# Adjacency build in runs of three chunks instead of four, with TensorE's run counts loaded once per tile

## The chip, the cores and the metric

One core of a Trainium2 chip runs the whole program. Its engines are TensorE (PE, with its weight loads shown as PEld), VectorE (DVE), ScalarE (ACT), GpSimd (POOL) and SyncE (SP), each with its own instruction stream; they meet by semaphores. The metric is the device time in microseconds (us), the median of three runs, lower is better.

## The reference

The reference is a two-layer graph network on 3125 nodes with 256 features: in each layer a graph convolution over 100000 edges, an attention mix and an expert block. The part that matters here is the sum over edges, which every graph convolution does with the same edge list:

```python
dst = jnp.minimum((3125 * jax.random.uniform(k, (100000,)) ** 2.0).astype(jnp.int32), 49999)
_o = jnp.argsort(dst, stable=True)
src, dst = src[_o], dst[_o]
...
deg = jax.ops.segment_sum(jnp.ones_like(dst, jnp.float32), dst, num_segments=n)
dinv = jnp.where(deg > 0, jax.lax.rsqrt(deg), 0.0)
msgs = h[src] * (dinv[src] * dinv[dst])[:, None]
return jax.ops.segment_sum(msgs, dst, num_segments=n)
```

The edges are sorted by target, and the targets are drawn from a square, so low targets have many more edges than high ones.

## The kernel before

The kernel does not gather rows edge by edge. It first builds the dense matrix of edge counts (3125 x 3125, one count for each pair of target and source), writes it to DRAM as `adjacency`, and later uses it in plain matrix products. The build is one stage, near the start, between two barriers of all engines.

The 100000 edges lie in 782 chunks of 128 edges, one edge per partition. The targets lie in 125 groups of 25 nodes, and five groups make one of 25 tiles. A group needs every chunk in which one of its targets occurs. Because edges are sorted, these chunks are neighbours, so a group has a first chunk and a count. The kernel works them off in runs of `RUN` chunks: a group has as many runs as its chunks need, rounded up, at least one. These numbers depend on the data; they are made on the chip and kept in `ranges_row` as four words for each group: first chunk, runs, runs of all groups before, runs up to and with this one. Each engine reads them into registers (`ranges_of`, L469) and loops over the runs.

For one chunk, two one-hot matrices are made: `hot_src` (128 edges x 125, the edge's source within its block, with a last column of ones) and `hot_key` (128 edges x 625, target within the group times source block). Their matrix product, 128x126 by 128x625 in two matmuls (512 and 113 columns), is added to the group's sums in PSUM. The engines split the work like this:

- POOL (L479) prepares the per-edge numbers of each run, `run_keys` and `run_srcs`, in a ring of 16 runs, so it may be 16 runs ahead.
- DVE (L501) makes `hot_key` for every chunk of a run and `hot_src` for all but the last. There is one slot per chunk of a run (`hot_src[:, j, :]`), and before slot j is written again TensorE must have used it (`hot_used`).
- ACT (L561) makes `hot_src` of the last chunk of a run in two operations, a square (L577) and a ReLU (L581), one group ahead of TensorE, and takes the sums of each finished group out of PSUM (`take_out`, L590).
- PE (L534) loads the group's words, waits until its PSUM bank is free, adds the self-loops with two matmuls (L545), and then does two matmuls for each chunk (L554).
- SP (L610) writes each group's counts to DRAM.

The order in each engine is as written. PSUM has four pairs of banks for five groups (`SUM_BANK`), and five buffers for the counts.

Of the kernel before, what the change touches and what calls it, by code (L numbers as in the profile page):

```python
# [15 lines left out]
ds = bass.ds  # L16
# [3 lines left out]
T = 25  # L20
P = N // T
G = 5
TG = T // G
# [2 lines left out]
HID = 512  # L26
E = 100000
CHUNKS = 782
RUN = 4
AHEAD = 16  # L30
CHUNKS_PAD = CHUNKS + RUN
GW = T * 25
# [14 lines left out]
OWNERS = 125  # L47
# [28 lines left out]
def graph_kernel(nc, a, out):  # L76
    with ExitStack() as top:
# [132 lines left out]
        with ExitStack() as phase:  # L210
# [9 lines left out]
            ranges_row = s("ranges_row", [1, OWNERS, 4], I32)  # L220
# [212 lines left out]
            with ExitStack() as build, nc.Block() as block:  # L433
# [35 lines left out]
                def ranges_of(engine, group):  # L469

                    why = "the ranges were clamped when they were made"
                    _, values = nc.values_load_multi_w_load_instructions(
                        ranges_row[0:1, ds(group, 1), :].rearrange("a g n -> a (g n)"), engines=[engine])
                    return (nc.s_assert_within(values[0], 0, CHUNKS, skip_runtime_bounds_check_because=why),
                            nc.s_assert_within(values[1], 1, CHUNKS // RUN + 1, skip_runtime_bounds_check_because=why),
                            values[2] & 0xFFFF,
                            values[3] & 0xFFFF)

                @block.gpsimd  # L479
                def _(pool):  # L480
                    with pool.Fori(0, T) as tile:
                        for k in range(TG):
                            group = tile * TG + k
                            first, runs, before, _ = ranges_of(mybir.EngineType.Pool, group)
                            with pool.Fori(0, runs) as i:
                                chunk = nc.s_assert_within(
                                    first + i * RUN, 0, CHUNKS_PAD - RUN, skip_runtime_bounds_check_because=(
                                        "a group's runs end with its last chunk, or a run after the first"))
                                n = before + i
                                at = nc.s_assert_within(n & (AHEAD - 1), 0, AHEAD - 1, skip_runtime_bounds_check_because=(  # L490
                                    "the mask leaves no other"))
                                alone(pool, hot_ready, n * RUN + RUN)
                                nc.gpsimd.tensor_tensor(
                                    run_keys[:, ds(at, 1), :].rearrange("p a j -> p (a j)"), edge_key[:, ds(chunk, RUN)],
                                    neg_group[:, ds(group, 1)].to_broadcast([128, RUN]), ALU.add).then_inc(run_made, 1)
                                nc.gpsimd.tensor_copy(run_srcs[:, ds(at, 1), :].rearrange("p a j -> p (a j)"),
                                                      src_low[:, ds(chunk, RUN)]).then_inc(run_made, 1)
                    pool.wait_ge(most_ready, 2)
                    nc.gpsimd.partition_all_reduce(deg_all[:], deg_most[:], 128, RMAX).then_inc(most_reduced, 1)
# [34 lines left out]
                @block.tensor  # L534
                def _(pe):
                    pe.sem_inc(hot_used, RUN)
                    with pe.Fori(0, T) as tile:
                        for k in range(TG):
                            group = tile * TG + k
                            _, runs, before, _ = ranges_of(mybir.EngineType.PE, group)  # L540
                            sums = psflat[0:P + 1, SUM_BANK[k] * 512:SUM_BANK[k] * 512 + GW]
                            pe.wait_ge(group_out, group + (TG + 1 - SUM_BACK[k]))

                            for b, e in ((0, 512), (512, GW)):
                                nc.tensor.matmul(sums[:, b:e], own_ident[0:P, k, :],  # L545
                                                 loop_blocks[0:P, ds(tile * -1 + (T - 1 + k * GW + b), e - b)],
                                                 start=True, stop=True, skip_group_check=True)
                            with pe.Fori(0, runs) as i:
                                for j in range(RUN):
                                    pe.wait_ge(hot_ready, (before + i) * RUN + (AHEAD * RUN + j + 1))  # L550
                                    if j == RUN - 1:
                                        pe.wait_ge(act_hot_ready, before + i + 2)
                                    for b, e in ((0, 512), (512, GW)):
                                        last = nc.tensor.matmul(sums[:, b:e], hot_src[:, j, :], hot_key[:, j, b:e],  # L554
                                                                start=False, stop=True, skip_group_check=True)
                                    last.then_inc(hot_used, 1)

                    pe.wait_ge(parts_summed, 1)
                    nc.tensor.transpose(ps[0:P, 7, 0:T], degree_row[:], ident[0:T, 0:T]).then_inc(deg_ready, 1)

                @block.scalar  # L561
                def _(act):
                    act.dma_start(xres[:], a["x"].rearrange("(t p) c -> p t c", p=P)).then_inc(x_landed, 16)
                    act.wait_ge(prepared, 2)
                    act.sem_inc(group_out, TG)
                    for k in range(TG):
                        act.sem_inc(stored[k], 16)

                    def make_sources(group):

                        first, runs, before, upto = ranges_of(mybir.EngineType.Activation, group)
                        with act.Fori(0, runs) as i:
                            act.wait_ge(act_hot_ready, before + i + 1)
                            chunk = nc.s_assert_within(
                                first + i * RUN + (RUN - 1), 0, CHUNKS_PAD - 1, skip_runtime_bounds_check_because=(
                                    "a group's runs end with its last chunk, or a run after the first"))
                            nc.scalar.activation(apart_sq[:], col_iota[:, 0:P], ACT.Square,  # L577
                                                 bias=src_low[:, ds(chunk, 1)], scale=-1.0).then_inc(squared, 1)
                            act.wait_ge(squared, before + i + 1)
                            act.wait_ge(hot_used, (before + i) * RUN + RUN)  # L580
                            nc.scalar.activation(hot_src[:, RUN - 1, 0:P], apart_sq[:], ACT.Relu,  # L581
                                                 bias=ones[:, 0:1], scale=-1.0).then_inc(act_hot_ready, 1)
                        return upto

                    def take_out(tile, k, upto):

                        group = tile * TG + k
                        act.wait_ge(stored[k], tile * 16 + 16)
                        alone(act, hot_used, upto * RUN + RUN)
                        nc.scalar.activation(counts[0:P + 1, k, :],  # L590
                                             psflat[0:P + 1, SUM_BANK[k] * 512:SUM_BANK[k] * 512 + GW],
                                             ACT.Copy, accum_out=row_edges[0:P + 1, ds(group, 1)]).then_inc(group_out, 1)

                    act.sem_inc(act_hot_ready, 1)
                    make_sources(0)
                    with act.Fori(0, T - 1) as tile:
                        for k in range(TG):
                            make_sources(tile * TG + k + 1)
                            _, _, _, upto = ranges_of(mybir.EngineType.Activation, tile * TG + k)
                            take_out(tile, k, upto)  # L600
                    for k in range(TG):
                        if k < TG - 1:
                            make_sources((T - 1) * TG + k + 1)
                        _, _, _, upto = ranges_of(mybir.EngineType.Activation, (T - 1) * TG + k)
                        take_out(T - 1, k, upto)
                    act.wait_ge(deg_ready, 1)

                    nc.scalar.activation(deg_sqrt[:], ps[0:P, 7, 0:T], ACT.Sqrt, bias=ones[0:P, 0:1]).then_inc(sqrt_ready, 1)
# [3057 lines left out]
```

## Time and profile before

| | |
|---|---|
| three runs | 4675.97, 4673.75, 4687.11 us; median 4675.97 |
| profiled execution, first to last instruction | 4665.5 us |
| median of the runs over that span | 10.5 us |
| the build stage, first to last L554 | about 571 us, 12% of the span |
| granted TensorE clock in that stage | 1.00 |
| runs / chunk places in the build | 276 / 1104 |

The page gives the profiled execution only as its span; the time outside the first and the last instruction is not in it, so spans are compared with spans and the difference is carried to the median. The stage is closed by a barrier on both sides, so what it gains or loses moves all that follows by as much.

### The profile page before, as it was taken

How to read it: one execution, taken by the hardware profiler on the slowest of the kernel's cores; microseconds unless marked ns; L12 is line 12 of the kernel's file. 1: busy time of each engine (PE TensorE's matmuls, PEld its weight loads, DVE VectorE, ACT ScalarE, POOL GpSimd, SP SyncE). 2: the span in 40 equal slices, each digit the busy share in tenths (PEclk: the TensorE clock that was granted, in tenths of full speed). 3: DMA queues.
4: the chain of work that ended last, by engine and by line, in shares of the span. 5: the costliest groups of instructions: out<-in, count | busy, mean ns of one | idle time of the engine just before them, and what ended most of it. 6: DMA issues, size and time to landing. Idle time of an engine off the chain costs nothing. (4 is left out here: it accounts for less than half of the span.)

```text
span 4665.5 us, 90783 instructions
## 1 busy us (share of the span) xinstructions
PE 3696.0 (79%) x23366; PEld 2634.7 (56%) x23367; DVE 2192.7 (47%) x5709; ACT 1348.5 (29%) x2983; POOL 739.5 (16%) x1224
## 2 busy tenths in 40 slices
PE   4888864899699989973464629859989899789998
PEld 2444433566388579651354416539879544457776
DVE  7888878888700221151263420270130677723333
ACT  2555532677700110320010203240000135233333
POOL 3222100000000000017423470200000466100000
PEclk9999975887799899986787859879999999989999
DMA  2111220323244024102010121224425100010000
GB/s 105 47 74 74 93 86 0 91 90 90 76 160 157 32 108 184 60 16 53 11 53 4 40 25 39 98 77 170 165 105 196 49 1 1 5 29 7 13 13 27
DMA packets 125733, 317.98 MB, mean 68 GB/s; under 512 B 43522, under 2 KB 76785, under 8 KB 111116
## 3 DMA queue, kind: packets, MB, share of 16 engines
q1 hardware_dynamic: 110404, 300.31, 18.5%
q0 software_dynamic: 11808, 9.68, 1.5%
q10 hardware_dynamic: 3404, 6.53, 0.4%
q8 instruction: 62, 1.02, 0.1%
q14 instruction: 55, 0.45, 0.0%
HBM read 244.21 MB, written 72.41 MB: 68 GB/s over the span
## 5 line engine op out<-in xcount | busy, mean ns | idle before, releaser
L554 PE MATMUL ps<-hot_key,hot_src 128*126 128x512 bf16 (+1 forms) x2208 | 416.9, 314 | 38.6 <-DVE hot_key L519 21.1
L519 DVE TENSOR_SCALAR hot_key<-col_iota,run_keys 128x625 bf16<-128x625 int16 x1104 | 393.7, 378 | 0.0
L2441 PE MATMUL ps<-xnT,ew 128*128 (+2 forms) x640 | 207.5, 479 | 206.7 <-issue 150.9
L1335 PE MATMUL ps<-gnn_u_thirds,near 125*128 125x256 bf16 x3000 | 334.7, 274 | 23.1 <-issue 23.1
L554 PEld LDWEIGHTS ps<-hot_key,hot_src 128*126 128x126 bf16 x2208 | 212.7, 136 | 234.2 <-DVE hot_key L519 171.7
L1335 PEld LDWEIGHTS ps<-gnn_u_thirds,near 125*128 125x128 bf16 x3000 | 329.7, 141 | 26.3 <-issue 24.7
L2441 PEld LDWEIGHTS ps<-xnT,ew 128*128 128x128 f32 x640 | 129.7, 210 | 279.2 <-issue 183.5
L2322 POOL DMA_INDIRECT rows_room<-node_table,src_idx x256 | 260.1, 1016 | 142.4 <-issue 142.4
L516 DVE TENSOR_SCALAR hot_src<-col_iota,run_srcs 128x125 bf16<-128x125 int16 x828 | 211.6, 256 | 97.4 <-PE ps L554 52.8
L863 PE MATMUL ps<-row_hot,slot_hot 128*128 128x512 f16 x1088 | 217.6, 351 | 3.1 <-DVE row_hot L1076 2.6
L2477 PE MATMUL ps<-table_thirds,rows_room 125*128 125x144 bf16 x1728 | 129.2, 232 | 113.9 <-issue 78.0
L2456 PE MATMUL ps<-ew,ehT 128*125 128x256 f32 x800 | 210.7, 409 | 0.0
L3620 DVE SCALAR_TENSOR_TENSOR xres<-ps,shares,xres 125x256 f32 x200 | 96.8, 484 | 239.5 <-PE ps L3585 218.6
L3574 PE MATMUL ps<-xnT,f 128*128 x640 | 185.5, 438 | 12.2 <-ACTq L3593 4.6
L1076 DVE TENSOR_SCALAR row_hot<-row_iota,row_of 128x670 f16<-128x670 int16 x544 | 189.4, 391 | 0.0
L2477 PEld LDWEIGHTS ps<-table_thirds,rows_room 125*128 125x128 bf16 x1728 | 114.2, 100 | 128.8 <-issue 128.4
L1335 PE MATMUL ps<-agg_u_thirds,near 125*128 125x257 bf16 x1500 | 175.4, 277 | 10.2 <-issue 9.7
L3574 PE MATMUL ps<-f_h1T,f 128*128 128x313 f32 (+1 forms) x640 | 180.1, 434 | 0.0
L3585 PE MATMUL ps<-fo,f_h2T 128*125 128x256 f32 x800 | 179.2, 379 | 0.0
L1335 PEld LDWEIGHTS ps<-agg_u_thirds,near 125*128 125x128 bf16 x1500 | 169.6, 141 | 16.6 <-issue 15.4
L1335 PE MATMUL ps<-gcn_u_thirds,near 125*128 125x256 bf16 x1500 | 166.6, 274 | 12.7 <-DVEq L1554 12.7
L3601 ACT ACTIVATE f_h1T<-ps,norm_shift,norm_scale 128x313 f32<-128x313 f32 (+1 forms) x160 | 98.0, 612 | 261.7 <-PE ps L3574 261.7
(570 smaller groups left out, 6651.9 us busy)
## 6 DMA issues: line engine op xcount, KB each, us to landing
near<-adjacency SPq DMA_DIRECT2D x80, 1562.5 KB, 6.6
adjacency<-counts SPq DMA_DIRECT2D x125, 312.5 KB, 2.2
own_in<-own_rows SPq DMA_DIRECT2D x34, 512.0 KB, 4.0
expert_rows<-rows_y SPq DMA_DIRECT2D x75, 125.0 KB
rows_room<-expert_rows SPq DMA_DIRECT2D x25, 375.0 KB
pair_in<-high_rows SPq DMA_DIRECT2D x34, 256.0 KB
pair_in<-low_rows SPq DMA_DIRECT2D x34, 256.0 KB
agg0a_adj<-adjacency SPq DMA_DIRECT2D x5, 1562.5 KB, 9.4
```

The costliest lines, as they stand in the source:

```text
L516: nc.vector.tensor_scalar(hot_src[:, j, 0:P], col_iota[:, 0:P], run_srcs[:, ds(at, 1), j:j + 1].rearrange("p a j -> p (a j)"), None, ALU.i ...
L519: nc.vector.tensor_scalar(hot_key[:, j, :], col_iota[:], run_keys[:, ds(at, 1), j:j + 1].rearrange("p a j -> p (a j)"), None, ALU.is_equal ...
L554: last = nc.tensor.matmul(sums[:, b:e], hot_src[:, j, :], hot_key[:, j, b:e], start=False, stop=True, skip_group_check=True)
L863: last = nc.tensor.matmul(ps[:, bank, 0:e - b], slot_hot[:, c % RING, :], row_hot[:, c % RING, b:e], start=False, stop=True, skip_group_ch ...
L1076: nc.vector.tensor_scalar(row_hot[:, c % RING, :], row_iota[:], row_of[i][:, c:c + 1], None, ALU.is_equal).then_inc(routes_made, 1)
L1335: last = nc.tensor.matmul(ps[:, j, 0:width], lead_tiles[BUF[j]][:, k, :], parts.thirds[:, k, i, :], start=(k == 0 and i == 0), stop=(k == ...
L2322: pool.indirect_dma_start(out=fetched[q][:, j, :], out_offset=None, in_=node_table, in_offset=bass.IndirectOffsetOnAxis(ap=src_idx[:, q, j ...
L2441: last = nc.tensor.matmul(ps[:, piece % 2, 0:n], w1[i][:, c, m * 128:(m + 1) * 128], xnT[:, c, ds(g * NG + first, n)], start=(c == 0), sto ...
L2456: last = nc.tensor.matmul(o, hT[:, c, j * P:(j + 1) * P], w2[i][:, c, :], start=False, stop=(c == 3))
L2477: last = nc.tensor.matmul(pick_bank(i, k, many)[:, slot * MIDS * HROW:(slot + 1) * MIDS * HROW], src_hot[i][0:P, tier, edges_of], table_th ...
L3574: last = nc.tensor.matmul(ps[:, piece % 2, 0:n], (w1, w2)[stage][i][:, c, m * 128:(m + 1) * 128], moving, start=(c == 0), stop=(c == 1))
L3585: last = nc.tensor.matmul(o, h2T[:, c, j * P:(j + 1) * P], wo[i][:, c, :], start=(c == 0), stop=(c == 1))
```

## The change

`RUN` goes from 4 to 3. With it go the number of slots for the one-hots (four to three), the share of ACT (one source one-hot in three, no longer in four), the number of runs of each group and the places that a group's chunks are rounded up to. TensorE reads its run counts no longer before each group but once for each tile, ten words in one load (`tile_runs_of`). ACT no longer loads the words of a group a second time before it takes the sums out: the count of all runs before group g + 1, which it has already, is the count up to group g.

```diff
-RUN = 4
+RUN = 3
...
+                def tile_runs_of(engine, tile):
+
+                    why = "the ranges were clamped when they were made"
+                    _, values = nc.values_load_multi_w_load_instructions(
+                        ranges_row[0:1, ds(tile * TG, TG), 1:3], engines=[engine])
+                    return [(nc.s_assert_within(values[2 * k], 1, CHUNKS // RUN + 1, skip_runtime_bounds_check_because=why),
+                             values[2 * k + 1] & 0xFFFF) for k in range(TG)]
...
                     with pe.Fori(0, T) as tile:
+                        counted = tile_runs_of(mybir.EngineType.PE, tile)
                         for k in range(TG):
                             group = tile * TG + k
-                            _, runs, before, _ = ranges_of(mybir.EngineType.PE, group)
+                            runs, before = counted[k]
...
-                        return upto
+                        return before
...
                         for k in range(TG):
-                            make_sources(tile * TG + k + 1)
-                            _, _, _, upto = ranges_of(mybir.EngineType.Activation, tile * TG + k)
-                            take_out(tile, k, upto)
-                    for k in range(TG):
-                        if k < TG - 1:
-                            make_sources((T - 1) * TG + k + 1)
-                        _, _, _, upto = ranges_of(mybir.EngineType.Activation, (T - 1) * TG + k)
-                        take_out(T - 1, k, upto)
+                            take_out(tile, k, make_sources(tile * TG + k + 1))
+                    for k in range(TG - 1):
+                        take_out(T - 1, k, make_sources((T - 1) * TG + k + 1))
+                    _, _, _, all_runs = ranges_of(mybir.EngineType.Activation, OWNERS - 1)
+                    take_out(T - 1, TG - 1, all_runs)
```

On TensorE, between the last chunk of a group and the first of the next group, the kernel before has (L554 is a chunk's matmul, L545 the self-loops' matmul, L548 the loop over runs, L472 the load of the words, ISA a register instruction):

```order
L554 MATMUL ps<-hot_key,hot_src 126x113
L548 REGISTER_ALU
L548 COMPARE_AND_BRANCH
L472 ISA
L472 TENSOR_LOAD ranges_row
L542 REGISTER_ALU
L545 ISA
L545 MATMUL ps<-loop_blocks,own_ident 126x512
L545 ISA
L545 MATMUL ps<-loop_blocks,own_ident 126x113
```

and the changed kernel, where lines stand nine further down (L563 is the chunk's matmul, L554 the self-loops'):

```order
L563 MATMUL ps<-hot_key,hot_src 126x113
L557 REGISTER_ALU
L557 COMPARE_AND_BRANCH
L551 REGISTER_ALU
L554 ISA
L554 MATMUL ps<-loop_blocks,own_ident 126x512
L554 ISA
L554 MATMUL ps<-loop_blocks,own_ident 126x113
```

Two instructions are gone, the address and the load; the load stands once, ahead of the first of five groups.

On ScalarE, from the last source one-hot of a group to the taking out of the group before it, the kernel before has (L581 the one-hot, L167 and L590 the waits and the copy):

```order
L581 ACTIVATE hot_src<-src_apart_sq,ones 128x125
L572 REGISTER_ALU
L572 COMPARE_AND_BRANCH
L472 TENSOR_LOAD ranges_row
L167 REGISTER_ALU
L167 ISA
L590 REGISTER_ALU
L590 ACTIVATE counts,row_edges<-ps 126x625
```

and the changed kernel:

```order
L590 ACTIVATE hot_src<-src_apart_sq,ones 128x125
L581 REGISTER_ALU
L581 COMPARE_AND_BRANCH
L167 REGISTER_ALU
L167 ISA
L599 REGISTER_ALU
L599 ACTIVATE counts,row_edges<-ps 126x625
```

The load between the two operations is gone.

## Rows read from the trace of the kernel before

**Rows 1.** The page: the costliest groups of the build stage.
```profile
L519 DVE TENSOR_SCALAR hot_key<-col_iota,run_keys 128x625 bf16<-128x625 int16 x1104 | 393.7, 378 | 0.0
L516 DVE TENSOR_SCALAR hot_src<-col_iota,run_srcs 128x125 bf16<-128x125 int16 x828 | 211.6, 256 | 97.4 <-PE ps L554 52.8
```

**Rows 2.** Windows: L554 over the stage (window, length, busy and count, clock, DMA).
```profile
59.00:630.70 571.70, 416.83 (x2208) 212.72 (x2208) 1.00 0.19 72
```

**Rows 3.** Windows: L545 over fifty groups of two runs (two matmuls a group).
```profile
257.05:471.34 214.29, 23.84 (x100) 12.87 (x100) 1.00 0.19 75
```

**Rows 4.** Timeline of PEld, two groups of two runs (start, length, [idle before]).
```profile
406.51 0.26 PEld L545 LDWEIGHTS ps<-loop_blocks,own_ident 125*126 125x126 bf16 x2 [1.20 <-issue]
407.05 1.01 PEld L554 LDWEIGHTS ps<-hot_key,hot_src 128*126 128x126 bf16 x8 [0.27 <-DVE hot_key L519]
408.46 0.19 PEld L554 LDWEIGHTS ps<-hot_key,hot_src 128*126 128x126 bf16 x2 [0.40 <-DVE hot_key L519]
409.73 0.19 PEld L554 LDWEIGHTS ps<-hot_key,hot_src 128*126 128x126 bf16 x2 [0.17 <-issue]
410.73 0.26 PEld L545 LDWEIGHTS ps<-loop_blocks,own_ident 125*126 125x126 bf16 x2 [0.81 <-issue]
411.26 1.01 PEld L554 LDWEIGHTS ps<-hot_key,hot_src 128*126 128x126 bf16 x8 [0.27 <-DVE hot_key L519]
```

**Rows 5.** Timeline of DVE in the same stretch.
```profile
407.85 0.26 DVE L516 TENSOR_SCALAR hot_src<-col_iota,run_srcs 128x125 bf16<-128x125 int16 x1 [1.10 <-PE ps L554]
408.31 0.25 DVE L516 TENSOR_SCALAR hot_src<-col_iota,run_srcs 128x125 bf16<-128x125 int16 x1
409.60 0.26 DVE L516 TENSOR_SCALAR hot_src<-col_iota,run_srcs 128x125 bf16<-128x125 int16 x1
412.06 0.26 DVE L516 TENSOR_SCALAR hot_src<-col_iota,run_srcs 128x125 bf16<-128x125 int16 x1 [0.71 <-POOL run_keys L493]
```

**Rows 6.** Timeline of PEld at the end: groups of one run.
```profile
625.33 1.02 PEld L554 LDWEIGHTS ps<-hot_key,hot_src 128*126 128x126 bf16 x8 [0.27 <-DVE hot_key L519]
626.72 0.26 PEld L545 LDWEIGHTS ps<-loop_blocks,own_ident 125*126 125x126 bf16 x2 [0.38 <-issue]
627.28 1.01 PEld L554 LDWEIGHTS ps<-hot_key,hot_src 128*126 128x126 bf16 x8 [0.30 <-DVE hot_key L519]
629.50 1.01 PEld L554 LDWEIGHTS ps<-hot_key,hot_src 128*126 128x126 bf16 x8 [0.27 <-issue]
```

**Rows 7.** Loads of words: L472, and one word at L1324 (ns min/median/max).
```profile
L472 ACTq TENSOR_LOAD <-ranges_row x250: 303/308/677, 49.9 to 630.6; - x125
L472 PEldq TENSOR_LOAD <-ranges_row x125: 328/334/533, 45.8 to 628.4; - x125
L472 PEldq FUSED_REGOPS  x100: 46/52/66, 91.6 to 628.3; - x100
L1324 PEldq TENSOR_LOAD <-many_edges x4: 306/315/323, 1282.6 to 3433.9; - x4
```

**Rows 8.** Timeline of ACT over one group of two runs.
```profile
404.58 0.69 ACT L590 ACTIVATE counts<-ps 126x625 f32<-126x625 f32 x1 [0.39 <-PE ps L554]
405.50 0.40 ACT L577 ACTIVATE src_apart_sq<-col_iota,src_low 128x125 bf16<-128x125 int16 x1
406.01 0.40 ACT L581 ACTIVATE hot_src<-src_apart_sq,ones 128x125 bf16<-128x125 bf16 x1
406.64 0.40 ACT L577 ACTIVATE src_apart_sq<-col_iota,src_low 128x125 bf16<-128x125 int16 x1 [0.22 <-ACT hot_src L581]
408.39 0.40 ACT L581 ACTIVATE hot_src<-src_apart_sq,ones 128x125 bf16<-128x125 bf16 x1 [1.36 <-PE ps L554]
409.18 0.69 ACT L590 ACTIVATE counts<-ps 126x625 f32<-126x625 f32 x1 [0.39 <-PE ps L554]
```

**Rows 9.** Timeline of POOL in the first group.
```profile
69.32 0.22 POOL L493 TENSOR_TENSOR run_keys<-edge_key,neg_group  x1 [0.66 <-DVE hot_key L519]
70.36 0.20 POOL L493 TENSOR_TENSOR run_keys<-edge_key,neg_group  x1 [0.68 <-DVE hot_key L519]
```

More of the change, by code:

```diff
@@ L569, in make_sources @@
                     def make_sources(group):
-                        first, runs, before, upto = ranges_of(mybir.EngineType.Activation, group)
+                        first, runs, before, _ = ranges_of(mybir.EngineType.Activation, group)
                         with act.Fori(0, runs) as i:
```

## The prediction

> **What bounds the kernel now.** I read the page first, then windows over the stage, then the waits and the timelines of its engines. Everything the change touches lies in one stage between two barriers; its 2208 matmuls lie in a window of 571.70 us at a granted clock of 1.00, the upper of the two levels (2.4 GHz) [rows 2]. So the forecast is the change of that window, and all that follows moves with it.
>
> No engine is full in it: VectorE works 394 us on `hot_key` and 212 us on `hot_src`, with overlap, and loses 97 us waiting before `hot_src`, most of it for TensorE [rows 1]. What repeats is a cycle through two engines. In a group of two runs TensorE's first chunk loads at 407.05; VectorE, which waited for that slot, starts the next run at 407.85, 0.80 later; the first chunk of that run loads at 408.46, 0.61 after VectorE's start; the last at 409.73, 1.88 after it; then TensorE needs 1.00 to the self-loops at 410.73 and 0.53 to the next first chunk at 411.26 [rows 4, 5]. The sum 0.80 + 1.88 + 1.00 + 0.53 is 4.21, the whole period of the group. While TensorE is between groups, VectorE has filled its slots and stands still. A further run in a group costs VectorE's own time, 407.85 to 409.60, 1.75 [rows 5]. The first group of a tile has 1.20 of idle time before its self-loops where others have 0.81, so 0.39 more [rows 4]; five groups then take 5 x 4.21 + 0.39 = 21.44, and fifty groups measure 214.29, 21.43 for five [rows 3]. A group of one run takes 1.95 or 2.22 [rows 6], I use 2.08.
>
> From the reference's edge list I count the chunks that each group touches. At four to a run that makes 276 runs, 1104 places, as in the trace [rows 1]: 25 groups of one run, 79 of two, 21 of more, with 51 runs beyond the second in all. The stage is then 100 x 4.21 + 25 x 2.08 + 51 x 1.75 + 24 x 0.39 = 421.0 + 52.0 + 89.3 + 9.4 = 571.6, against 571.7 measured. The same sum can be made for the changed kernel.
>
> **The change part by part.** Counts: at three to a run there are 345 runs, 1035 places. No group has one run any more: 84 have two, 41 have more, with 95 runs beyond the second.
>
> VectorE's run: one chunk with a source one-hot falls out, 407.85 to 408.31, 0.46 [rows 5]; its own time for a run is 1.75 - 0.46 = 1.29. The last chunk of a run comes 1.88 - 0.46 = 1.42 after its start.
>
> Slots: there are three, and the first is free again only by the round trip shown above: 0.61 from VectorE's start to TensorE's load, 0.80 from there to VectorE's next start, 1.41 together [rows 4, 5]. Under 1.75 that was hidden; over 1.29 it is not. A further run costs 1.41, a gain of 0.34 a run, but 0.47 for a chunk place where it was 0.44. The bounds are 1.29 and 1.75, and I take 1.41 since both halves are read from rows.
>
> TensorE's load: between groups the address (0.05) and the load (0.33) go [rows 7], 0.39 with rounding; the idle time there is 0.81 [rows 4], of which branch, wait and address of the self-loops stay. I take 0.50, 0.11 over the two durations for the sequencer's gaps, an estimate; the bounds are 0.39 and 0.81. The period of a group of two runs is 4.21 - 0.46 - 0.50 = 3.25. At the start of a tile the load stays, so that 0.50 is not saved there. It fetches ten words instead of four. One word takes 0.315 and four take 0.334 [rows 7], 0.006 a word, so I add 0.04; if the whole load grew with the words it would be 0.84, 0.50 more. A tile start costs 0.39 + 0.50 + 0.04 = 0.93 over 3.25.
>
> The Trainium skill, page "Runtime: NRT & Kernel Launch", section "Instruction fetch mechanics", says that such a load takes about 200 ns for each register. By it the ten words would take 2.0 us, and the sum would be some 39 us higher; four words would take 0.8, and the trace has 0.334.
>
> ScalarE: its cycle for a group of two runs without waits is, from taking out at 404.58, 0.92 to the square, 0.51, 0.63, again 0.51 to the second ReLU, and 0.79 (408.39 to 409.18) to the next taking out, 3.36 [rows 8]. For one run it is 0.92 + 0.51 + 0.79 = 2.22, just what the last one-run groups take [rows 6], so the chain is real. Without the load (0.31, with a gap 0.35, out of an idle time of 0.39 ahead of the taking out [rows 7, 8]) it is 3.01, below 3.25: ScalarE follows. If none of the load's time comes back it is 3.36, and 84 groups lose 0.11 each, +9 us; if it does, nothing. I take nothing, since the idle time before L590 has room for the load only. The freed 0.24 a group is all its slack; three-run groups have 3.01 + 1.14 = 4.15 against 4.66.
>
> GpSimd makes a run in 1.04 (69.32 to 70.36) [rows 9], below 1.41, and may be 16 runs ahead; even with one 0.32 load a group two runs fit into 3.25. SyncE's writes stay 125, at least 3.25 apart and into buffers five groups old. The shorter clearing of `hot_src` and the column fewer in the preparation lie beside GpSimd's start, at nothing; were they in the open it would be 0.2 us.
>
> The sum: 125 x 3.25 + 95 x 1.41 + 24 x 0.93 = 406.3 + 134.0 + 22.3 = 562.5, against 571.6: -9.1 us. Where it comes from: 59 groups keep two runs, -0.96 each, -57; 25 go from one to two, +1.17, +29; 20 go from two to three, +0.45, +9; 21 longer ones, -4; 24 tile starts, +0.54, +13. The large gain on the common group is mostly eaten by groups that need one run more. With 4665.5 for the span this gives 4656.4; the median of the runs lies 10.5 above the span, so 4676 becomes 4667.
>
> **Rivals.** A: three slots cost nothing, a further run takes 1.29. For it: TensorE catches up between runs with 0.27 a chunk when nothing is missing. Against it: 0.80 and 0.61 are in every group. Price 95 x -0.12 = -11, so 4656.
>
> B: ScalarE becomes the bound, as computed, +9, so 4676, no change. For it: it makes 345 pairs of operations instead of 276 and has 0.24 of slack a group; a slower start after a taking out (404.58 to 405.50) would use that up. Against it: the idle time of 1.36 before its ReLU [rows 8].
>
> C, the other side: TensorE's load was beside other work and its removal gives nothing between groups. In one-run groups the idle time before the self-loops is 0.38, not 0.81 [rows 6], so there the load partly ran beside earlier matmuls. If it saved nothing in two-run groups either, 101 groups get 0.50 less, +50: 4717. It passes +0.3% when less than 0.27 is saved. Against it: in the two-run groups before, TensorE's sequencer waits with the last chunk for VectorE, so the load comes after it, and that stays so after the change.
>
> D: the load of ten words is dear. Growing with the words, +0.46 x 24 = +11 over my sum: 4678. It would need 0.96 more a tile, 1.3 us for the load, to make the kernel slower by 0.3%; the skill's rule quoted above would reach that.
>
> That the change doesn't do what it says I rule out: the order of instructions shows one load a tile on TensorE and three chunks a run.
>
> **How the numbers follow.** A measurement of this kernel tells about 0.3%, 14 us, from no change. My forecast (4667) has 0.52, A 0.17, B 0.16, C 0.06, D 0.05, and 0.04 for none of these. Forecast, B and the weak form of D read as no change, though the forecast may fall 5 us lower by the bounds of the load and the spread of medians: 0.10 of its chance goes to faster. A is faster save for 0.03, and half of the rest. That is 0.26 faster, 0.65 same, 0.09 slower. The range starts below A, at 4652, for a saving of more than 0.50 a group, and ends at 4682, above B and D in its weak form with a few us of spread; C is left out.
>
> **What would show it.** `hot_key` 1035 times, the ReLU 345 times. First chunk to first chunk 3.25 in groups of two runs, 4.2 at a tile start, 1.41 between VectorE's runs inside a long group with a wait for TensorE of about 0.1 before each `hot_src`. Idle time before the self-loops about 0.3 inside a tile; TensorE's load about 0.37 us, 25 times. No wait of the matmuls for ScalarE's one-hot beyond a few us. The stage ends at about 622 instead of 631, and the stages after it keep their lengths. A period of 3.4 or more with matmuls waiting for ScalarE is B; an idle time of 0.8 before the self-loops is C; a load above 1 us is D. A shift of the later stages by more than the stage's would make the prediction wrong in a way that it doesn't cover.

## The result and the profile after

The changed kernel takes 4753.27 us (median; 4749.77 to 4753.61), the kernel before 4678.43 in the same comparison (4673.75 to 4687.11): a ratio of 1.0158, 95% interval 1.0139 to 1.0176. It is slower by 75 us. The forecast was 4667, no change. (One further execution of the changed kernel took 8075 us and is left out as disturbed.)

The spans of the two profiled executions are 4751.2 and 4665.5 us. In the changed kernel the stage's chunk matmuls are in line 563, the self-loops in 554, TensorE's load of a tile's counts in 482. The window of line 563 over the stage (columns: length, PE busy and count, PEld busy and count, granted clock, DMA share, GB/s):

```profile
59.00:707.00 648.00, 448.08 (x2069) 222.78 (x2070) 0.88 0.16 63
```

The answer to [rows 2]: the last chunk ends at about 707, not at 630.7, so the stage is 76 us longer, and the granted clock in it is 0.88 where it was 1.00. The two spans differ by another 9 us, in pieces of up to 4 us over the later stages. The span of the traced execution lies 2 us below the median of the runs in the changed kernel, but 13 us below it in the kernel before. So the medians differ by 75, which is what the stage alone gives; that the 9 us come from the change isn't shown.

The stage's costliest groups and the loads of words, to be read against [rows 1, 7]. A load's three times are its shortest, median and longest in ns:

```profile
L563 PE MATMUL ps<-hot_key,hot_src 128*126 128x512 bf16 (+1 forms) x2070 | 448.4, 346 | 67.8 <-DVE hot_key L527 60.9
L527 DVE TENSOR_SCALAR hot_key<-col_iota,run_keys 128x625 bf16<-128x625 int16 x1035 | 363.5, 379 | 0.0
L524 DVE TENSOR_SCALAR hot_src<-col_iota,run_srcs 128x125 bf16<-128x125 int16 x690 | 177.3, 257 | 209.4 <-PE ps L563 162.8 <-POOL run_srcs L504 18.2 <-issue 9.2
```
```profile
L472 ACTq TENSOR_LOAD <-ranges_row x126: 305/308/528, 49.4 to 706.1; - x126
L472 POOLq TENSOR_LOAD <-ranges_row x125: 315/323/545, 45.1 to 673.6; - x125
L482 PEldq TENSOR_LOAD <-ranges_row x25: 2715/2912/2962, 45.4 to 687.1; - x25
```

VectorE does less work than before (364 us on keys, 177 on sources) and waits three times as long for TensorE, 163 us where it was 53. The last row names the main cause: the load of ten words takes 2.91 us, not 0.37. The waits of the stage (us in total, times, longest) show it as "issue" ahead of the self-loops, the longest 3.8 us where it was 1.2 [rows 4]:

```profile
PEld ps L554 <- issue: 116.8, 124, 3.8
PE ps L554 <- issue: 83.5, 24, 3.6
DVE hot_src L524 <- PE ps L563: 162.8, 148, 4.4
```

Now the timeline of PEld over two groups of two runs and the start of a tile, to be read against [rows 4]:

```profile
409.60 0.26 PEld L554 LDWEIGHTS ps<-loop_blocks,own_ident 125*126 125x126 bf16 x2 [0.31 <-issue]
...
412.82 0.30 PEld L554 LDWEIGHTS ps<-loop_blocks,own_ident 125*126 125x126 bf16 x2 [0.26 <-issue]
...
416.09 0.26 PEld L554 LDWEIGHTS ps<-loop_blocks,own_ident 125*126 125x126 bf16 x2 [0.26 <-issue]
...
418.90 0.19 PEld L563 LDWEIGHTS ps<-hot_key,hot_src 128*126 128x126 bf16 x2 [0.18 <-issue]
422.77 0.31 PEld L554 LDWEIGHTS ps<-loop_blocks,own_ident 125*126 125x126 bf16 x2 [3.68 <-issue]
423.36 0.29 PEld L563 LDWEIGHTS ps<-hot_key,hot_src 128*126 128x126 bf16 x2 [0.27 <-issue]
423.84 0.34 PEld L563 LDWEIGHTS ps<-hot_key,hot_src 128*126 128x126 bf16 x2 [0.20 <-issue]
```

Between groups the idle time before the self-loops fell from 0.81 to 0.26 and the period from 4.21 to 3.22 and 3.27, as forecast. At the tile start it is 3.68 and the period 6.68. After it TensorE's own pace changes: one chunk follows the other by 0.48 us (423.36 to 423.84), where the kernel before needs 0.27 when nothing is missing. Windows of line 563 from ahead of this idle time to just past its end, right behind it, and after that (the last one holds the next tile start too):

```profile
403.00:424.00 21.00, 14.20 (x63) 7.09 (x63) 0.83 0.20 76
423.30:427.00 3.70, 3.56 (x12) 1.92 (x12) 0.50 0.00 0
427.00:444.00 17.00, 10.20 (x49) 5.05 (x49) 0.90 0.24 94
```

The granted clock is 0.50, the lower of the two levels (1.2 GHz), right behind it. It falls so at all 24 tile starts. The next two groups take 3.80 to 3.85 and 3.4 to 3.6 us instead of 3.25; over the tiles that is 0.7 to 1.1 us more, in the median 0.87.

So there are two losses a tile: the load, 2.91 - 0.37 = 2.54, and the clock behind it, 0.87. The forecast's sum with these is 562.5 + 24 x 2.54 + 24 x 0.87 = 644.3, against 647.9 measured, first chunk to last.

### The profile page after: what moved, and what is told of

The parts are those of the page before. It is cut to its first block and busy times, and to the rows that moved or that the text cites. A ratio compares the mean times of both kernels' runs of the same rounds, so it can differ in the third digit from the quotient of the medians.

```text
span 4751.2 us, 91780 instructions
## 1 busy us (share of the span) xinstructions
PE 3737.7 (79%) x23228; PEld 2655.9 (56%) x23229; DVE 2160.4 (45%) x5502; ACT 1404.6 (30%) x3121; POOL 760.3 (16%) x1362
## 5 line engine op out<-in xcount | busy, mean ns | idle before, releaser
L563 PE MATMUL ps<-hot_key,hot_src 128*126 128x512 bf16 (+1 forms) x2070 | 448.4, 346 | 67.8 <-DVE hot_key L527 60.9
L563 PEld LDWEIGHTS ps<-hot_key,hot_src 128*126 128x126 bf16 x2070 | 222.8, 151 | 282.4 <-DVE hot_key L527 198.0
L527 DVE TENSOR_SCALAR hot_key<-col_iota,run_keys 128x625 bf16<-128x625 int16 x1035 | 363.5, 379 | 0.0
L524 DVE TENSOR_SCALAR hot_src<-col_iota,run_srcs 128x125 bf16<-128x125 int16 x690 | 177.3, 257 | 209.4 <-PE ps L563 162.8
L590 ACT ACTIVATE hot_src<-src_apart_sq,ones 128x125 bf16<-128x125 bf16 x345 | 139.1, 403 | 190.8 <-PE ps L563 167.6
```

Of the source, the lines that this page charges most:

```text
L524: nc.vector.tensor_scalar(hot_src[:, j, 0:P], col_iota[:, 0:P], run_srcs[:, ds(at, 1), j:j + 1].rearrange("p a j -> p (a j)"), None, ALU.i ...
L527: nc.vector.tensor_scalar(hot_key[:, j, :], col_iota[:], run_keys[:, ds(at, 1), j:j + 1].rearrange("p a j -> p (a j)"), None, ALU.is_equal ...
```

## The experiments

They ran on other chips of the same kind, where the kernel before takes 4305 to 4312 us, so each is compared by its ratio to before on the same chip, or by the end of the stage in its trace. The stage of before ends at the same time there: in the third experiment, which is before up to the last group, the first thing behind that group starts at 630.7. In eight of the nine experiments that were timed the median moves by what the stage does, within about 5 us (the other, by 8).

**The load alone is undone.** The changed kernel, with TensorE loading the four words of a group in each group again.

```diff
-                        counted = tile_runs_of(mybir.EngineType.PE, tile)
...
-                            runs, before = counted[k]
+                            _, runs, before, _ = ranges_of(mybir.EngineType.PE, group)
```

> The changed kernel (runs of three) with TensorE's words loaded before each group again, four words each. Theory 1 (the ten-word load of 2.9 us and the half clock after it are the loss): both go; each group pays the 0.50 of its own load again. Stage 125 x 3.75 + 95 x 1.45 + 24 x 0.40 = 616 us, granted clock 1.00 in it, so about 4722, 45 above before and 30 below the changed kernel. Theory 2 (runs of three themselves are the loss, by hand-overs and the end of one-run groups): the stage stays near 648 and the time near 4753.

4347.28 against 4305.21, ratio 1.0098 (1.0081 to 1.0115); the stage ends at 674.5, 44 us later than before. Three self-loops from PEld's timeline, the first of them a tile start, and the window of line 562, the chunk matmuls' line here, over the stage:

```profile
407.51 0.26 PEld L553 LDWEIGHTS ps<-loop_blocks,own_ident 125*126 125x126 bf16 x2 [1.21 <-issue]
...
411.23 0.29 PEld L553 LDWEIGHTS ps<-loop_blocks,own_ident 125*126 125x126 bf16 x2 [0.77 <-issue]
...
414.99 0.26 PEld L553 LDWEIGHTS ps<-loop_blocks,own_ident 125*126 125x126 bf16 x2 [0.78 <-issue]
```
```profile
59.00:674.50 615.50, 411.08 (x2069) 199.29 (x2070) 1.00 0.17 67
```

Periods of 3.75, which is 3.25 plus the 0.50 of the load, idle times of 0.8 and 1.2 as before, and a clock of 1.00 but for one short stretch. The forecast's sum with the 0.50 given back at 101 more groups is 125 x 3.75 + 95 x 1.41 + 24 x 0.43 = 613, and 615.3 is measured. So the rest of that sum was sized nearly right, and three chunks to a run, without the cheaper counts, cost 44 us. The first theory holds, the second is out.

**The load alone is done.** The kernel before with the tile's load and nothing else.

```diff
...
+                        counted = tile_runs_of(mybir.EngineType.PE, tile)
...
-                            _, runs, before, _ = ranges_of(mybir.EngineType.PE, group)
+                            runs, before = counted[k]
```

> The kernel before (runs of four) with the ten-word load once a tile and nothing else. Theory 1: 0.50 saved in 101 groups, 24 tile starts with 2.57 us more load, 0.50 not saved, and about 0.9 of half-clock matmuls after it: 571.6 - 50.5 + 24 x 4.0 = 617 us of stage, about 4723, and the clock falls to 0.5 after each load. Theory 2: the load lies beside other work with four slots, stage about 525 to 571, 4630 to 4678, clock 1.00.

4356.52, ratio 1.0119 (1.0102 to 1.0136); the stage ends at 677.2, 46 later.

```profile
L482 PEldq TENSOR_LOAD <-ranges_row x25: 2698/2857/2967, 45.2 to 662.1; - x25
```

Groups of two runs take 3.71 (4.21 less 0.50, as forecast), a tile start 7.15, and the group behind it 4.70; the clock falls at all 24 tile starts. The load that saves 0.50 a group costs more than it saves at four chunks to a run too.

**What a load costs by its words.** The kernel before with ten single loads on TensorE behind its last group: 1, 2, 4, 5, 8 and 10 words that lie side by side, then 2, 4, 8 and 10 words of which two in every four are taken, as the changed kernel takes them.

```diff
+                    words = ranges_row[:].rearrange("a g n -> a (g n)")
...
+                    _, got = nc.values_load_multi_w_load_instructions(words[0:1, 0:4], engines=[mybir.EngineType.PE])
+                    alone(pe, group_out, (sum(got[1:], got[0]) & 15) + 1)
...
+                    _, got = nc.values_load_multi_w_load_instructions(ranges_row[0:1, 0:5, 1:3], engines=[mybir.EngineType.PE])
+                    alone(pe, group_out, (sum(got[1:], got[0]) & 15) + 1)
```

> The kernel before, with loads of words on TensorE added after the last group, when it only waits: 1, 2, 4, 5, 8 and 10 words that lie side by side, then 2, 4, 8 and 10 words taken as two of every four. Theory A (by count): both series alike, 0.32 to 0.34 up to four words and 2.9 for ten, with a step or a slope between. Theory B (by gaps): side by side stays below 0.4 up to ten, and two of every four is dear already at four words. The time of the kernel changes by less than 15 us.

In the order in which they were named (ns, and when); each row is a single load:

```profile
L559 PEldq TENSOR_LOAD <-ranges_row x1: 318/318/318, 630.7 to 630.7; - x1
L561 PEldq TENSOR_LOAD <-ranges_row x1: 552/552/552, 631.5 to 631.5; - x1
L563 PEldq TENSOR_LOAD <-ranges_row x1: 572/572/572, 632.5 to 632.5; - x1
L565 PEldq TENSOR_LOAD <-ranges_row x1: 891/891/891, 633.7 to 633.7; - x1
L567 PEldq TENSOR_LOAD <-ranges_row x1: 587/587/587, 635.1 to 635.1; - x1
L569 PEldq TENSOR_LOAD <-ranges_row x1: 1090/1090/1090, 636.3 to 636.3; - x1
L571 PEldq TENSOR_LOAD <-ranges_row x1: 543/543/543, 638.1 to 638.1; - x1
L573 PEldq TENSOR_LOAD <-ranges_row x1: 1026/1026/1026, 639.1 to 639.1; - x1
L575 PEldq TENSOR_LOAD <-ranges_row x1: 1978/1978/1978, 640.7 to 640.7; - x1
L577 PEldq TENSOR_LOAD <-ranges_row x1: 2447/2447/2447, 643.3 to 643.3; - x1
```

Two words in every four: each word after the first costs (2447 - 318) / 9 = 237 ns. Side by side, eight words cost 587, hardly more than four, and ten cost 1090, two words at 0.25 more. Neither theory holds as it stands: ten words side by side are cheaper than ten with gaps, but not below 0.4. The words seem to be fetched one by one, unless four or eight lie together; that is a reading of ten single loads. The Trainium skill, page "Runtime: NRT & Kernel Launch", section "Instruction fetch mechanics", gives some 200 ns for each register: by the scattered rows of this trace that holds (237), by the rows of four and eight side by side it does not.

**The ten words side by side.** The changed kernel with a packed copy of the two columns that TensorE needs.

```diff
...
+                    step(nc.vector.tensor_copy(counts_row[:], ranges_row[:, :, 1:3]))
...
-                        ranges_row[0:1, ds(tile * TG, TG), 1:3], engines=[engine])
+                        counts_row[0:1, ds(tile * TG, TG), :].rearrange("a g n -> a (g n)"), engines=[engine])
```

> The changed kernel, but the two words of each group are copied once into a table of their own, so that the ten words of a tile lie side by side. Theory (the load costs by separate pieces, and the half clock comes from the long idle time of TensorE): the load takes about 1.1 us instead of 2.9, the clock stays 1.00, and a tile start falls by 1.8 and the two groups after it by 0.87 together: stage 648 - 24 x 2.7 = 584, some 12 above before. Rival (the clock falls with any tile-start load): only 1.8 goes, stage 605, 33 above before. Second rival (the count of words sets the load): nothing changes, 75 above before.

4362.06 against 4312.26, ratio 1.0117 (1.0101 to 1.0132), +50: better than the changed kernel, but between the two rivals (+33 and +75) and far from the theory (+12). The loads of two neighbouring tiles, even and odd, and the idle time that each leaves:

```profile
L484 PEldq TENSOR_LOAD <-counts_row x1: 1431/1431/1431, 391.7 to 391.7; - x1
```
```profile
L484 PEldq TENSOR_LOAD <-counts_row x1: 2775/2775/2775, 410.9 to 410.9; - x1
```
```profile
393.36 0.31 PEld L556 LDWEIGHTS ps<-loop_blocks,own_ident 125*126 125x126 bf16 x2 [2.26 <-issue]
413.91 0.31 PEld L556 LDWEIGHTS ps<-loop_blocks,own_ident 125*126 125x126 bf16 x2 [3.61 <-issue]
```

They alternate so through all 25 tiles, 1.28 to 1.60 and 2.78 to 2.92. A tile's words begin at 40 bytes times its number, so every odd tile begins off a multiple of 16 bytes. Its load costs as much as words read singly.

**The table padded.** Twelve words a tile instead of ten, so that every tile begins on a multiple of 16 bytes (the lines are set against the experiment before).

```diff
-            counts_row = s("counts_row", [1, OWNERS, 2], I32)
+            counts_row = s("counts_row", [1, T, 12], I32)
...
+                        counts_row[0:1, ds(tile, 1), 0:2 * TG].rearrange("a t n -> a (t n)"), engines=[engine])
```

> The changed kernel with its ten words of a tile side by side in a table of twelve words a tile, so that each tile's words begin on a multiple of 16 bytes. Theory (reads are of aligned sets of words, odd tiles of the packed table began off such a multiple): every one of the 25 loads takes what the even tiles took there, 1.1 to 1.6 us, tile-start periods 5.0 to 5.3 us, stage 571.7 - 9 + 24 x (1.3 - 0.37) = 585 us where the clock stays at the upper level, and up to 600 where it still falls after the idle of a tile start: time before + 13 to + 28 us. Rival (the two lengths alternate for another reason, such as which half of the table is read): they still alternate between 1.3 and 2.9, and the time stays at + 50 us.

4349.84 against 4312.12, ratio 1.0083 (1.0066 to 1.01), +38. All loads are of the short kind now, so the alignment was the cause, and not which half of the table is read:

```profile
L485 PEldq TENSOR_LOAD <-counts_row x25: 1286/1533/1591, 45.7 to 649.3; - x25
```

But the time is 10 above the theory's upper end. PEld's timeline at a tile start, and the windows of line 566, each about one tile long:

```profile
423.51 0.30 PEld L557 LDWEIGHTS ps<-loop_blocks,own_ident 125*126 125x126 bf16 x2 [2.41 <-issue]
424.06 0.28 PEld L566 LDWEIGHTS ps<-hot_key,hot_src 128*126 128x126 bf16 x2 [0.24 <-issue]
424.54 0.34 PEld L566 LDWEIGHTS ps<-hot_key,hot_src 128*126 128x126 bf16 x2 [0.20 <-issue]
```
```profile
385.00:404.00 19.00, 12.72 (x60) 6.33 (x60) 0.91 0.21 83
404.00:423.00 19.00, 12.63 (x60) 6.36 (x60) 0.91 0.22 86
423.00:442.00 19.00, 13.86 (x60) 6.93 (x60) 0.82 0.20 77
```

An idle time of 2.4 us is followed by the lower clock (weight loads of 0.28 to 0.34 instead of 0.19) nearly as surely as one of 3.7 is: at 21 of 24 tile starts. The three others, at 216, 321 and 345 us, are a control within the run: the next group of three runs takes 4.66 to 4.73 there, as any such group at the upper clock, and 5.2 to 5.6 where the clock falls around the tile start. An idle time of 1.2 is followed by it at none of 24 tile starts in the kernel before and at 1 of 24 in the first experiment. A tile now pays 1.53 - 0.37 = 1.16 for the load and 0.55 to 0.9 for the clock (the next periods are 3.80 and 3.26, or 3.50 and 3.60): 24 x 1.7 - 9 = +32, and +38 is measured. That can't be told from the first experiment (+42): even side by side and aligned, the ten words gain little or nothing over the four small loads in their place.

**Loads moved off the path.** The kernel before, where TensorE loads the words of the next group right behind the first chunk of a run.

```diff
+                        _, runs, before, _ = ranges_of(mybir.EngineType.PE, tile * TG)
...
-                            _, runs, before, _ = ranges_of(mybir.EngineType.PE, group)
...
+                                    if j == 0 and k < TG - 1:
+                                        _, next_runs, next_before, _ = ranges_of(mybir.EngineType.PE, group + 1)
+                            runs, before = next_runs, next_before
```

> The kernel before with TensorE loading the words of the next group after the first chunk of every run, where it waits for VectorE, not between groups (the first group of a tile keeps its load ahead). Theory 1 (what counts is that no load stands between a group's last chunk and the next first one): groups of two runs take 4.21 - 0.50 = 3.71, one-run groups are bound by ScalarE at 2.22, stage about 100 x 3.71 + 25 x 2.2 + 89 + 9 = 524, about 4631. Rival: the load inside the run delays the later chunks and VectorE's slots by as much as it saves, stage 560 to 580, about 4678.

4275.93 against 4305.21, ratio 0.9937 (0.992 to 0.9953): 29 us faster, the stage by 27, between the theory (-47) and the rival (none). Groups of two runs take 3.67 to 3.75, so the 0.50 comes back in most of them, but the first of each tile takes 3.95. There the self-loops of the tile's second group wait for ScalarE, which takes the last group of the tile before out of the PSUM banks that the two share. At 22 of 24 tile starts they begin 0.13 to 0.15 after the end of that. The end of the taking out, and the self-loops:

```profile
410.37 0.19 ACT L593 ACTIVATION_READ_ACCUMULATOR counts<-ps  x1
```
```profile
410.69 0.26 PEld L545 LDWEIGHTS ps<-loop_blocks,own_ident 125*126 125x126 bf16 x2 [0.39 <-issue]
```

**The same at three chunks to a run.** The first experiment with the early load:

```diff
...
+                                    if j == 0 and k < TG - 1:
+                                        _, next_runs, next_before, _ = ranges_of(mybir.EngineType.PE, group + 1)
```

> Runs of three, ScalarE as in the changed kernel, and TensorE loads the words of the next group after the first chunk of every run. Theory (by the sum of the prediction, with 1.45 for a further run): 125 x 3.25 + 95 x 1.45 + 24 x 0.9 = 566, about 6 below before. Rival (with runs of three there is too little waiting in a run to hide a load of 0.4, and ScalarE has 0.2 a group): groups of two runs take 3.4 to 3.6, stage 585 to 610, 13 to 38 above before.

4332.05 against 4312.26, ratio 1.0048 (1.0033 to 1.0064), the stage 22 longer than before. Two-run groups take 3.4 or 3.6, not 3.25, and three-run groups 4.9 to 5.2, not 4.66. The rival has the number: the load is hidden in part only, and it is paid again in a further run. Whether the shorter run or ScalarE's small slack is the reason wasn't separated.

**The tile's load early, from the padded table.** TensorE's loop over five parts of five tiles written out; in a part the next tile's ten words are loaded in a tile's last group, between self-loops and first chunk.

```diff
...
+                            if k == TG - 1 and at < 5 * TG - 1:
+                                counted = tile_runs_of(mybir.EngineType.PE, tile + 1)
                             with pe.Fori(0, runs) as i:
```

> The padded table, and TensorE's loop over five parts of five tiles written out; in a part, the next tile's words are loaded in the last group of a tile, between its self-loops and its first chunk, not at the tile's start. Theory (nothing of the load is waited for, since VectorE is behind then): 20 of 24 tile starts cost what another group costs, the two-run groups stay at 3.25 us, so the sum of the forecast, -9, less 20 x 0.93 = -28 us, and 4 exposed starts at + 1 us each: about -24 us. Rival (the load of 1.1 to 1.3 us holds up TensorE, which is what makes buffers free for VectorE): the last group of each tile is longer by the load, the clock falls behind it as at the tile start, and the time is that of the padded table less the branch, 0 to + 15 us.

4336.43 against 4312.12, ratio 1.0051 (1.0032 to 1.007), +24. Nothing of the load is hidden. PEld's timeline around it, then one further group:

```profile
414.85 0.26 PEld L559 LDWEIGHTS ps<-loop_blocks,own_ident 125*126 125x126 bf16 x2 [0.26 <-issue]
417.07 0.74 PEld L570 LDWEIGHTS ps<-hot_key,hot_src 128*126 128x126 bf16 x6 [1.96 <-issue]
...
419.77 0.27 PEld L559 LDWEIGHTS ps<-loop_blocks,own_ident 125*126 125x126 bf16 x2 [0.28 <-issue]
420.35 0.74 PEld L570 LDWEIGHTS ps<-hot_key,hot_src 128*126 128x126 bf16 x6 [0.32 <-DVE hot_key L530]
```

The first chunk is 1.68 later than without the load, and that group takes 4.92 where others take 3.25. TensorE's first chunk is what frees the buffer for VectorE, so a stop ahead of it is in the cycle of the whole group. The clock falls around 18 of the 20 early loads too. The rival's mechanism is right; its +0 to +15 was too low.

**ScalarE's part.** The early load at four chunks to a run, and ScalarE's second load taken out as the change does it.

```diff
-                            make_sources(tile * TG + k + 1)
-                            _, _, _, upto = ranges_of(mybir.EngineType.Activation, tile * TG + k)
-                            take_out(tile, k, upto)
+                            take_out(tile, k, make_sources(tile * TG + k + 1))
```

> Runs of four with TensorE's early load, and ScalarE without its second load as in the changed kernel. Theory (ScalarE bounds only the one-run groups, 2.22 to 1.87, and some first groups of a tile): 3 to 9 us below the kernel with the early load alone, 31 to 38 below before. Rival (the ScalarE part gives nothing): 28 below before, as without it.

4282.03 against 4312.26, ratio 0.9932 (0.9918 to 0.9945), -30, what the early load gives without it (-29), so the rival holds. The trace shows that it does move something: the first group of a tile takes 3.74 now instead of 3.95, but the next takes 3.94 instead of 3.74, the tile start 4.73 instead of 4.60, and the clock falls at three tile starts. Why the gain is lost again in the next group stays open.

**Five tiles written out.** The same with TensorE's loop over five parts of five tiles, so that the early load and the missing branch reach 20 of 24 tile starts.

```diff
-                    with pe.Fori(0, T) as tile:
+                    with pe.Fori(0, T // 5) as part:
...
-                                    if j == 0 and k < TG - 1:
+                                    if j == 0 and at < 5 * TG - 1:
```

> As the last one, with TensorE's loop over 25 tiles made a loop over 5 parts of 5 tiles each, written out, so that 20 of 24 tile starts have no load and no loop branch between groups. Theory: each of the 20 saves 0.88, 17 us, about 50 below before. Rival (the written-out loop of 600 instructions has to be fetched at its branches, and stalls as much as it saves): 28 to 38 below before or above it.

4273.64 against 4312.26, ratio 0.9918 (0.9904 to 0.9931): 39 us faster, the fastest version here, ahead of both kernels. A tile start inside a part takes 3.9 to 4.0, where the kernel before takes 4.6. The groups take 3.7 to 3.95, though, not 3.7 throughout. The load stands between a run's first and second chunk, so the second chunk is late and frees its buffer late. VectorE's first two source one-hots of a run show it:

```profile
388.18 0.26 DVE L516 TENSOR_SCALAR hot_src<-col_iota,run_srcs 128x125 bf16<-128x125 int16 x1
...
388.88 0.26 DVE L516 TENSOR_SCALAR hot_src<-col_iota,run_srcs 128x125 bf16<-128x125 int16 x1
```

They are 0.70 apart where they were 0.46 [rows 5]. Whether this is what keeps the groups above 3.7 wasn't tried by itself.

## Why the prediction was wrong

The step that failed is the price of the ten-word load: "One word takes 0.315 and four take 0.334 [rows 7], 0.006 a word, so I add 0.04". The load took 2.91, not 0.37. The two rows were for reads of another kind: a single word, and four words side by side on a multiple of 16 bytes. The change reads two words of every four. The third experiment measures those at 0.237 for each further word, and the padded table shows that the same ten words cost 1.5 when they lie together and aligned. The prediction bounded this load at 0.84 from rows that could not bound it, and gave the case "the load is dear" a chance of 0.05. Its own sign, "a load above 1 us is D", is what the profile shows. The Trainium skill's 200 ns a register (page "Runtime: NRT & Kernel Launch", section "Instruction fetch mechanics"), which the prediction set aside for the four-word row, was the better guide for words that don't lie together.

The second part of the loss was in no case of the prediction: [rows 2] gave a clock of 1.00, and a longer idle time of TensorE was counted as idle time alone. It costs 0.87 a tile on top. No experiment changed the clock and left the idle time as it was; the three tile starts of the padded table are the nearest to that.

Point by point:

- A group of two runs at 3.25: right. The trace has 3.22 to 3.27 where the clock is at its upper level, and with the group's load back 3.75. The load between groups was worth 0.50, as estimated, so rival C is out.
- A further run at 1.41, bound by three buffers: right in its mechanism, and nearly so in size, 1.41 in groups of three runs and 1.45 in longer ones. VectorE's starts and TensorE's first chunks in a long group of the changed kernel:

```profile
76.82 0.26 DVE L524 TENSOR_SCALAR hot_src<-col_iota,run_srcs 128x125 bf16<-128x125 int16 x1 [0.16 <-POOL run_srcs L504]
...
78.27 0.27 DVE L524 TENSOR_SCALAR hot_src<-col_iota,run_srcs 128x125 bf16<-128x125 int16 x1
...
79.72 0.26 DVE L524 TENSOR_SCALAR hot_src<-col_iota,run_srcs 128x125 bf16<-128x125 int16 x1
```
```profile
77.46 0.19 PEld L563 LDWEIGHTS ps<-hot_key,hot_src 128*126 128x126 bf16 x2 [0.48 <-DVE hot_key L527]
...
78.92 0.19 PEld L563 LDWEIGHTS ps<-hot_key,hot_src 128*126 128x126 bf16 x2 [0.48 <-DVE hot_key L527]
```

  From VectorE's start to TensorE's load it is 0.64 (0.61 in the prediction), and from there to VectorE's next start 0.81 (0.80). Rival A (1.29) is out.
- The counts, 1035 and 345: right. That the gain of common groups is eaten by groups that need one more run is right too: with the load kept as it was, three chunks to a run are 44 us slower, and the forecast's sum gives 41.
- ScalarE follows, rival B out: right. The weight loads waited 4.9 us in all for its one-hot.
- The start of a tile at 4.18: wrong, 6.68, with 0.87 behind it; 24 x (2.50 + 0.87) = 81, which turns -9 into +72, against 76.
- Later stages keep their lengths: right within 4 us each, 9 us together in the two traces.
- The median 10.5 above the span: not a constant of the kernel. The changed kernel's median lies 2 above its span, so the trace of before seems to be of a short execution.

## What to carry to other kernels

A load of words into registers is priced by where the words lie, not by their number alone: look at the address pattern of the row that you take the price from, and if it isn't the new one's, the row is no bound. If several small loads are gathered into one, lay the words side by side on a 16-byte boundary; here even that did not beat the small loads. Prefer to move a small load behind work that nobody waits for: all three faster versions rest on that. When a change lengthens an idle time of TensorE, price the lower clock behind it as well.

## What was not expected of the hardware

- Words two in every four: 0.318 us for the first and 0.237 for each more. Eight side by side: 0.587. The same ten packed words: 1.3 to 1.6 from a multiple of 16 bytes, 2.8 to 2.9 from elsewhere. Four words take 0.334 in the groups' loop but took 0.572 as a single load behind it; that difference stays open.
- How often an idle time of TensorE was followed by the lower clock: one of 3.5 to 3.9 us at all 24 tile starts, in the changed kernel and in the second experiment; one of 2.3 to 2.5 at 21 of 24 (padded table); one of 2.0 ahead of a first chunk at 18 of 20 (the tile's load early; not at 417.07 above); one of 0.8 to 1.4 at none of 24 in the kernel before and with the early load at four chunks, at 1 of 24 in the first experiment, and at 3 of 24 each with the early load at three chunks and without ScalarE's load. It stays for one to two groups. What decides at the shorter ones stays open.
- Of an early load TensorE hides only what its buffers don't need: behind a run's first chunk the 0.33 us were hidden in most groups at four chunks to a run, in part at three, and ahead of the first chunk nothing of 1.5 us.
